# A mixture-of-experts layer on one core: rows kept in token order and fetched by a table, in place of rows scattered into expert order

## The chip, the core and the metric

The kernel runs on one core of a Trainium2 chip. The core has TensorE (PE in the profile; PEld is its weight load), VectorE (DVE), ScalarE (ACT), GpSimd (POOL) and SyncE (SP), each with its own instruction stream; they meet only at semaphores. 16 DMA engines serve all queues. The metric is the device time of one execution in microseconds; a kernel is compared by the median of its runs.

## What is computed

One layer: causal attention over a batch of 4 sequences of 1024 tokens and 256 channels, then a mixture of 8 experts. The part that matters here, with N = 4096 tokens:

```python
x = x + layernorm(attention(layernorm(x)))
xf = layernorm(x).reshape(-1, 256)
w, idx = top_k(xf @ Wg, 2);  w = softmax(w)              # two experts for each token
xhat = (xf - mean(xf)) * rsqrt(var(xf) + 1e-6)
h = relu((xhat * gamma[e] + beta[e]) @ W1[e] + b1[e])    # for each expert e
out[e] = h @ W2[e] + b2[e] + xf
y = sum over the token's two experts of w * out[e]
x = x + layernorm(y)
```

## The kernel before

The program is a row of stages, `project`, `attend`, `route` and `experts`, each a block at whose end all engines wait for one another. Everything that the change touches is in `route` and `experts`.

`route` works through the 4 sequences, called batches b, each of 8 tiles of 128 tokens (t). DVE takes the moments of the attention's output (L1034, L1038), POOL turns them into a reciprocal root and a shift with a power (`roots`, L997 to L1003), ACT applies these (`norm_y`, L1187), DVE adds the residual (L1044) and takes moments again, normalises into `xb` (`normalise`, L1053) and takes moments a third time. PE turns each tile (L1227), ACT copies it out of PSUM (`xfT`, L1195), PE multiplies it with the gate's weights (L1232). `pick_experts` on DVE (L1074 to L1098) finds each token's two experts, PE counts with triangular matmuls how many earlier tokens chose the same expert (`ps_r`, L1237 to L1242), and DVE gets each row's slot in the DRAM buffer `xs`. There each expert has a region of N + 256 rows. POOL then scatters the normalised rows `xh` into these slots: `scatter`, L1011, one indirect DMA of 128 rows for each tile and choice, 64 in all, cut in threes between the roots. Each row carries two more words: its token and the second expert. SP at last writes rows of zeros behind each expert's last row (L981), when the counts are known. DVE meanwhile works out how many tiles of 256 rows each expert has and where each begins in `xs` (L1148 to L1176: `base`, `tile_row`).

`experts` runs over the tiles i of 256 rows, expert after expert, 36 in this run. Tile i: SP has fetched its rows with one plain DMA (L1342) two tiles ahead, PE turns them (`turn`, L1464), ACT and DVE split them in two parts, PE does the first layer (L1477, 48 matmuls), turns the rows of the next tile, and does the second layer (L1488, 48 matmuls). DVE adds the bias into `o` (L1560), POOL reads the two extra words (L1407), works out each row's place in `ys` (L1416 to L1423), scatters `o` with two indirect DMAs (L1430) and waits for them to land. When an expert is done, SP refills the weights that it had used with the next but one expert's: `fill`, L1360, four DMAs of 1 MB. Every engine that loops reads nine loop bounds from `base` first (`firsts`, L1322). A last part reads `ys` back in token order and mixes.

The order is written by hand. POOL's queue in the routing holds roots and scatters in turn; SP's queue in `experts` holds the fetches and the refills.

## Time and profile before

| | us |
|---|---|
| median of 3 runs | 1285.25 (1284.64 to 1285.45) |
| the profiled execution's own time | 1283.42 |
| its span | 1281.8 |
| attention ends, routing begins | at 633.5 |
| experts' block begins | at 782.7 |
| first matmul of an expert | at 792.0 |
| last matmul of an expert | at 1215.6 |
| a tile of 256 rows | 11.72 |

In the rows, a line of the timeline is: start in us from the span's start, duration, engine, line of the kernel, operation, written tile <- read tiles, shapes, count, and in brackets the time for which the engine was idle before it and what ended that. An engine called SPq or POOLq is the queue's own record. A line of the groups has the busy time and the mean duration in ns of one. The granted clock of TensorE is 1.00 at 2.4 GHz and 0.50 at 1.2 GHz.

### The profile page before, as it was taken

The page shows a single profiled execution, that of the slowest core. Times are in us where ns is not written, and L with a number is a line of the kernel's source. Part 1 is how long each engine was busy: PE and PEld are TensorE (multiplying, and loading weights), DVE is VectorE, ACT ScalarE, POOL GpSimd, SP SyncE. Part 2 cuts the span into 40 slices and gives each one's busy share as a digit, 9 for nine tenths or more (in the row PEclk, how much of TensorE's full clock was granted, in tenths as well). Part 3 has the DMA queues.
Part 4 walks back from the last instruction along what each step waited for, and adds up shares of the span by engine and source line. Part 5 has one row for each costly group of instructions (what it writes and reads, how often), then busy time and mean ns, then how long its engine had stood idle before and what let it go on. Part 6 is the DMA issues. An engine that isn't in the chain of part 4 may idle for free. (4 is left out here: it accounts for less than half of the span.)

```text
span 1281.8 us, 24447 instructions
## 1 busy us (share of the span) xinstructions
PE 1054.5 (82%) x7329; PEld 806.4 (63%) x7329; DVE 824.1 (64%) x2492; ACT 640.9 (50%) x1111; POOL 588.2 (46%) x675
## 2 busy tenths in 40 slices
PE   5979999999999999998533513999999999999900
PEld 2545555555555555554233513999999999999900
DVE  6739877777777777772188521556655655565577
ACT  2640666666666666666444422444444544454533
POOL 4214555555555555556747771223222222232237
PEclk9985999999999999999855555999999999999955
DMA  4994344545444444432261235142541414421173
GB/s 147 372 359 131 107 167 167 167 167 167 165 165 160 159 160 160 169 113 108 96 236 66 83 128 196 59 162 63 183 178 48 177 49 177 146 79 50 41 270 131
DMA packets 93849, 190.03 MB, mean 148 GB/s; under 512 B 27480, under 2 KB 58600, under 8 KB 85512
## 3 DMA queue, kind: packets, MB, share of 16 engines
q1 hardware_dynamic: 84508, 165.14, 37.0%
q0 software_dynamic: 7680, 22.09, 5.0%
q10 hardware_dynamic: 1588, 1.92, 0.5%
q8 instruction: 34, 0.56, 0.2%
q14 instruction: 39, 0.32, 0.1%
HBM read 109.54 MB, written 79.05 MB: 147 GB/s over the span
## 5 line engine op out<-in xcount | busy, mean ns | idle before, releaser
L778 ACT ACTIVATE att_pt<-att_ps_s 128x1024 f32<-128x1024 f32 (+3 forms) x384 | 297.9, 814 | 180.5 <-PE att_ps_s L693 176.8
L805 DVE CUSTOM_DVE_ANT_0 att_ps_m<-att_ps_m,keep_future 128x384 f32<-128x384 f32 (+2 forms) x384 | 204.3, 586 | 77.9 <-PE att_ps_m L656 77.9
L1521 ACT ACTIVATE moe_hf<-moe_ps_h,moe_b 128x256 f32<-128x256 f32 x288 | 134.4, 474 | 224.7 <-PE moe_ps_h L1477 215.3
L656 PE MATMUL att_ps_m<-att_k,att_q 128*128 128x512 f32 (+3 forms) x576 | 181.1, 389 | 5.1 <-DVE att_pm L805 3.9
L814 DVE TENSOR_REDUCE att_pm<-att_ps_m 128x1 f32<-128x512 f32 x256 | 161.4, 685 | 21.8 <-PE att_ps_m L656 21.7
L601 POOL TENSOR_SCALAR_AFFINE_SELECT att_pt<-att_pt 128x512 f32<-128x512 f32 x128 | 81.3, 636 | 186.8 <-ACT att_pt L778 186.8
L693 PE MATMUL att_ps_s<-att_q,att_k 128*128 128x512 f32 (+3 forms) x576 | 156.0, 360 | 6.3 <-ACT att_pt L778 5.2
L1430 POOL DMA_INDIRECT ys<-moe_o,moe_home x72 | 74.1, 1029 | 183.3 <-DVE moe_o L1560 170.4
L693 PEld LDWEIGHTS att_ps_s<-att_q,att_k 128*128 128x128 f32 x576 | 95.2, 188 | 56.5 <-issue 28.9
L1554 DVE TENSOR_TENSOR moe_hTl<-moe_hf,moe_hTh 128x256 fp32r<-128x256 f32 x288 | 124.1, 431 | 10.0 <-DVE moe_hTh L1552 0.2
L656 PEld LDWEIGHTS att_ps_m<-att_k,att_q 128*128 128x128 f32 x576 | 99.7, 195 | 47.9 <-DVE att_pm L805 15.1
L591 POOL TENSOR_TENSOR att_rec<-att_sums,att_minus 128x16 f32<-128x16 f32 x33 | 95.9, 2905 | 31.8 <-ACT att_sums L764 31.8
L710 PE MATMUL att_ps_o<-att_pt,att_v 128*17 128x512 f32 (+3 forms) x1152 | 107.1, 488 | 3.7 <-ACTq L746 3.1
L1552 DVE CAST moe_hTh<-moe_hf 128x256 fp32r<-128x256 f32 x288 | 84.3, 293 | 33.1 <-ACT moe_hf L1521 29.5
L1560 DVE TENSOR_TENSOR moe_o<-moe_ps_o,moe_b 128x256 f32<-128x256 f32 x72 | 27.2, 419 | 110.0 <-PE moe_ps_o L1488 110.0
L1477 PE MATMUL moe_ps_h<-moe_xTh,weights_w_0h 128*128 128x256 f32 x288 | 81.7, 284 | 5.4 <-issue 5.4
L1488 PE MATMUL moe_ps_o<-moe_w2h,moe_hTh 128*128 128x256 f32 x288 | 82.0, 285 | 0.0
L1488 PE MATMUL moe_ps_o<-weights_w_0h,moe_hTh 128*128 128x256 f32 x288 | 82.0, 285 | 0.0
L1477 PE MATMUL moe_ps_h<-moe_xTh,weights_w_0l 128*128 128x256 f32 x288 | 81.5, 283 | 0.0
L1477 PE MATMUL moe_ps_h<-moe_xTl,weights_w_0h 128*128 128x256 f32 x288 | 81.5, 283 | 0.0
L1477 PE MATMUL moe_ps_h<-moe_xTh,moe_w1l 128*128 128x256 f32 x288 | 80.9, 281 | 0.0
L1477 PE MATMUL moe_ps_h<-moe_xTl,moe_w1h 128*128 128x256 f32 x288 | 80.9, 281 | 0.0
(197 smaller groups left out, 2503.8 us busy)
## 6 DMA issues: line engine op xcount, KB each, us to landing
att_raw<-in_w SPq DMA_DIRECT2D x16, 1024.0 KB, 5.3
ws<-att_raw_hi SPq DMA_DIRECT2D x16, 1024.0 KB, 3.9
ws<-att_raw SPq DMA_DIRECT2D x16, 1024.0 KB, 5.8
moe_rows<-xs SPq DMA_DIRECT2D x38, 258.0 KB
att_q<-qs SPq DMA_DIRECT2D x33, 256.0 KB
att_k<-ks SPq DMA_DIRECT2D x66, 128.0 KB
weights_w_0h<-ws SPq DMA_DIRECT2D x8, 1024.0 KB
weights_w_0l<-ws SPq DMA_DIRECT2D x8, 1024.0 KB
```

Of the source, the lines that this page charges most:

```text
L591: pool.tensor_tensor(rec[:, c], got[:, :, :, HS], minus[:], ALU.pow).then_inc(rec_done, 1)
L656: ins = pe.matmul(out[:, end - keys:end], qg[slot][:, h // 2, i * P:(i + 1) * P], kg[slot][:, h, k0:k0 + keys], start=not whole, stop=not ...
L693: ins = pe.matmul(out[:, e, off:CH], kg[slot][:, 2 * p + e, j * P:(j + 1) * P], qg[slot][:, p, c * CH + off:(c + 1) * CH], start=True, sto ...
L710: ins = pe.matmul(ps_o[32 * h:32 * h + VW, off:CH], vg[slot][:, j, h * VW:(h + 1) * VW], pt[:, blk % NPT, h, off:CH], start=(j == 0), stop ...
L778: act.activation(pt[:, blk % NPT, 2 * p:2 * p + 2, off:CH], ps_s[k % 2][:, :, off:CH], ACT.Exp, scale=HS ** -0.5).then_inc(ex_done, 1)
L805: ins = dve.tensor_tensor_reduce(part, part, future[:, CH - keys:CH], 1.0, LOWEST, ALU.add, ALU.max, pm[:, g % 2, 0, head, place:place + 1])
L814: return dve.tensor_reduce(pm[:, g % 2, 0, h, place:place + 1], src, AX.X, ALU.max)
L1477: ins = pe.matmul(ps_h[f % NHB][:], w1[r][a][:, k, f * P:(f + 1) * P], xT[m][:, k], start=(n == 0), stop=(n == 3 * CT - 1))
L1488: ins = pe.matmul(ps_o[t][:], hT[a][:, f, t * P:(t + 1) * P], w2[r][m][:, f], start=(f == 0 and (a, m) == pieces[0]), stop=(f == FT - 1 an ...
L1521: act.activation(hf[:, f % NHB], ps_h[f % NHB][:], ACT.Relu, bias=b1[r][:, f:f + 1]).then_inc(hf_done, 1)
L1552: dve.tensor_copy(hT[0][:, f], hf[:, f % NHB]).then_inc(hh_done, 1)
L1554: dve.tensor_tensor(hT[1][:, f], hf[:, f % NHB], hT[0][:, f], ALU.subtract).then_inc(hl_done, 1)
```

## The change

Rows are kept in token order. ACT writes `xh` as before, but SP stores it with one plain DMA for each batch in `xs`, now N + 128 rows of 256 words (the last 128 are zeros). No row is scattered in the routing and no region is padded.

In place of that, a table tells for each slot of each expert which row belongs there. Each expert has 34 columns of 128 slots (`TABLE`), 272 in all. A row's rank among its expert's rows is split on DVE into `low` (the last seven bits, the partition) and `high` (the column). For each tile and choice, `make_low` compares the numbers 0 to 127 with `low` (a one-hot row of 128 for each token), and `make_block` compares 0 to 271 with `cell`, the column. Both are done by POOL, 16 + 16 instructions for each batch; of the last batch DVE does the 16 of `make_low` and 8 of the 16 of `make_block`. ACT multiplies the first by the row's number in two parts (`rows_of`: 2 activations of 1024 columns and 8 of 256 for each batch), and PE adds up 32 matmuls of 272 columns for each batch in one PSUM bank (`table`). At the end DVE turns the sum into `home` (where the result goes) and `token` (which row to fetch), in 6 instructions.

In `experts`, POOL fetches the rows: it loads the tile's column number into a register, copies two columns of `token`, and gathers with two indirect DMAs (`gather`). It does so for tile i + 2 ahead of the scatter of tile i. SP no longer fetches, and its refills follow each other in its queue.

The routing is also rearranged: the second normalisation's moments are derived from the first (DVE's `normalise` and its third `moments` are gone; ACT does both normalisations in `norm_x`, straight from the head tiles), the copy L1204 is gone, moments are taken two batches ahead, and the loops over batches are written out.

POOL's queue in the routing. Before, around the last batches' roots:

```order
L1003 TENSOR_TENSOR route_shift<-route_nmean,route_rstd 128x8
L1011 DMA xs<-route_xh,route_slot 34816x258 x11
L997 TENSOR_SCALAR route_veps<-route_mv 128x8
L999 TENSOR_SCALAR route_nmean<-route_mv 128x8
L1001 TENSOR_TENSOR route_rstd<-route_veps,route_mhalf 128x8
L1003 TENSOR_TENSOR route_shift<-route_nmean,route_rstd 128x8
L1011 DMA xs<-route_xh,route_slot 34816x258 x27
```

After, from the roots of batch 2's `norm_y` to those of batch 3's:

```order
L1024 TENSOR_TENSOR route_shift<-route_nmean,route_rstd 128x8
L963 TENSOR_SCALAR route_at_low<-route_cols,route_low 128x128 x16
L969 TENSOR_SCALAR route_at_block<-route_cols,route_cell 128x272 x16
L1031 TENSOR_SCALAR route_veps<-route_mv 128x8
L1032 TENSOR_SCALAR route_veps<-route_mv 128x8
L1034 TENSOR_SCALAR route_nmean<-route_mv 128x8
L1036 TENSOR_TENSOR route_rstd<-route_veps,route_mhalf 128x16
L1038 TENSOR_TENSOR route_shift<-route_nmean,route_rstd 128x16
L1019 TENSOR_SCALAR route_veps<-route_mv 128x8
L1020 TENSOR_SCALAR route_nmean<-route_mv 128x8
L1022 TENSOR_TENSOR route_rstd<-route_veps,route_mhalf 128x8
```

The scatters behind a batch's roots have become comparisons, 16 and 16, and the roots of the next two normalisations stand behind them. On ACT `rows_of` of batch b stands behind `norm_y` of batch b + 3 and ahead of `norm_x` of batch b + 2.

SP's queue at the start of `experts`. Before:

```order
L1342 DMA moe_rows<-xs 128x2x258
L1338 TENSOR_LOAD keep_tile_row
L1338 ISA x2
L1342 ISA
L1342 DMA moe_rows<-xs 128x2x258
L1351 DMA moe_b<-in_b 128x8
L1353 DMA moe_b<-in_b 128x256
L1360 DMA moe_w1h<-ws 128x2048
```

After:

```order
L1410 DMA moe_b<-in_b 128x8
L1412 DMA moe_b<-in_b 128x256
L1419 DMA moe_w1h<-ws 128x2048
L1419 DMA moe_w1l<-ws 128x2048
L1419 DMA moe_w2h<-ws 128x2048
```

The two fetches that stood ahead of the second expert's weights on SP are now gathers on POOL; nothing stands ahead of the weights but the biases.

POOL's queue in one tile of the experts' loop, from the wait for the turned rows on. Before:

```order
L1416 TENSOR_SCALAR moe_chosen<-moe_tag,keep_ei 128x2
L1418 ISA
L1420 TENSOR_TENSOR moe_place<-moe_chosen,moe_tag 128x2
L1421 REGISTER_ALU
L1423 CAST moe_home<-moe_place 128x2
L1424 REGISTER_ALU
L1405 ISA
L1407 COPY moe_tag<-moe_rows 128x4
L1427 ISA
L1430 DMA ys<-moe_o,moe_home 8704x256 x2
L1432 ISA
```

After (the copy of `home`, with a register load of its own, stands ahead of these):

```order
L1480 REGISTER_ALU
L1482 ISA
L1456 ISA
L1456 TENSOR_LOAD keep_tile_row
L1456 ISA x2
L1462 ISA
L1462 COPY moe_source<-keep_token 128x2
L1463 REGISTER_ALU
L1466 DMA moe_rows<-xs,moe_source 128x256 x2
L1485 ISA
L1488 DMA ys<-moe_o,moe_home 8704x256 x2
L1490 REGISTER_ALU
```

The gather now stands ahead of the tile's scatter, and behind the wait for the scatter of the tile before, which closes the loop's body.

The diff, cut to its core:

```diff
+        def make_low(eng, b):
+
+            if b > 0:
+
+                eng.wait_ge(rows_done, b * LOW_ROWS)
+            for k in range(K):
+                for t in range(TB):
+                    ins = eng.tensor_scalar(at_low[:, k, t], cols[:, 0:P], low[:, k, t:t + 1], None, ALU.is_equal)
+            ins.then_inc(low_done, 1)
+
+        def make_block(eng, k):
+
+            for t in range(TB):
+                ins = eng.tensor_scalar(at_block[:, k, t], cols[:], cell[:, k, t:t + 1], None, ALU.is_equal)
+            ins.then_inc(block_done, 1)
...
-                sp.wait_ge(homes, 2)
-                sp.wait_ge(pad_known, 1)
-                settle(sp, keep["passed"])
-                for e in range(E):
-                    row = sp.value_load(pad[0:1, e:e + 1], min_val=e * CAP, max_val=e * CAP + N)
-                    sp.dma_start(d["xs"][bass.ds(row, XT), :].rearrange("(k p) c -> p k c", p=P),
-                                 zeros[:]).then_inc(padded, 16)
-                sp.wait_ge(padded, 16 * E)
+                sp.dma_start(d["xs"][N:N + P, :], zeros[:]).then_inc(kept, 16)
+                for b in range(B):
+                    sp.wait_ge(xh_done, b + 1)
+                    sp.dma_start(d["xs"][b * T:(b + 1) * T, :].rearrange("(k p) c -> p k c", p=P),
+                                 xh[:, b * TB:(b + 1) * TB]).then_inc(kept, 16)
+                sp.wait_ge(kept, 16 * (B + 1))
...
-                roots(0, 0)
-                roots(1, 1)
-
-                cuts = (0, 5, 10, K * TB)
-                for b in range(-1, B - 1):
-                    for n, (norm, ahead) in enumerate(((0, 2), (2, 1), (1, 2))):
-                        if b + ahead < B:
-                            roots(norm, 3 * (b + 1) + 2 + n if b + 2 < B else 3 * B - 1)
-                        if b >= 0:
-                            scatter(b, cuts[n], cuts[n + 1])
-                scatter(B - 1, 0, K * TB)
-                pool.wait_ge(scattered, 16 * K * TILES)
...
+                def table(b):
+
+                    pool.wait_ge(parted, b + 1)
+                    if b < B - 1:
+                        make_low(pool, b)
+                    if b > 0:
+
+                        pool.wait_ge(tabled, b)
+                    for k in range(K if b < B - 1 else K // 2):
+                        make_block(pool, k)
+
+                roots_y(0)
+                roots_y(1)
+                roots_x(0)
+                roots_x(1)
+                pool.wait_ge(c_in, 16 * 9)
+                for b in range(B):
+                    if b + 2 < B:
+                        roots_y(b + 2)
+                    table(b)
+                    if b + 2 < B:
+                        roots_x(b + 2)
...
-                        ins = dve.tensor_tensor(hit[:, k], pick[:, k], place[:], ALU.mult)
+                        ins = dve.tensor_tensor(hit[:, k], pick[:, k], ps_r[:], ALU.mult)
                     then(ins)
-                    then(dve.tensor_reduce(slot_f[:], hit[:], AX.X, ALU.add))
-                    dve.tensor_copy(slot[:, :, bass.ds(b * TB, TB)], slot_f[:]).then_inc(slots_in, 1)
+                    then(dve.tensor_reduce(rank[:], hit[:], AX.X, ALU.add))
+                    then(dve.tensor_copy(rank_i[:], rank[:]))
+                    then(dve.tensor_scalar(rank_i[:], rank_i[:], P.bit_length() - 1, None, ALU.logical_shift_right))
+                    then(dve.tensor_copy(high[:], rank_i[:]))
+                    if b > 0:
+
+                        dve.wait_ge(low_done, b)
+                        dve.wait_ge(block_done, b * K)
+                    dve.scalar_tensor_tensor(low[:], high[:], float(-P), rank[:], ALU.mult, ALU.add)
+                    then(dve.scalar_tensor_tensor(cell[:], which[:], float(TABLE), high[:], ALU.mult, ALU.add))
+                    dve.nop().then_inc(parted, 1)
                     then(dve.tensor_reduce(part[:], taken[:].rearrange("p t e -> p e t"), AX.X, ALU.add))
...
+                dve.wait_ge(tabled, B)
+                table = ps_tab[:, 0:E * TABLE]
+                then(dve.tensor_scalar(free[:], table, 0.0, None, ALU.is_equal))
+                then(dve.tensor_tensor(spare[:].rearrange("p (n k) -> p n k", k=2), free[:].rearrange("p (n k) -> p n k", k=2),
+                                       own_row[:, K:2 * K].unsqueeze(1).to_broadcast([P, E * TABLE // 2, 2]), ALU.mult))
+                then(dve.scalar_tensor_tensor(keep["home"][:], table, -1.0, spare[:], ALU.add, ALU.add))
+                then(dve.tensor_copy(token_i[:], keep["home"][:]))
+                then(dve.tensor_scalar(token_i[:], token_i[:], K.bit_length() - 1, None, ALU.logical_shift_right))
+                then(dve.tensor_copy(keep["token"][:], token_i[:]))
...
+                def norm_x(b):
+                    act.wait_ge(x_rs, b + 1)
                     settle(act, keep["passed"])
                     for t in range(TB):
-                        act.activation(by_group(yn, t), head_tile(b, t), ACT.Identity, scale=rstd[:, 0, t:t + 1],
-                                       bias=shift[:, 0, t:t + 1]).then_inc(yn_done, 1)
-
-                def keep_batch(b, call):
+                        act.activation(by_group(xf, b * TB + t), head_tile(b, t), ACT.Identity, scale=rstd[:, b, 1, t:t + 1],
+                                       bias=shift[:, b, 1, t:t + 1]).then_inc(xf_done, 1)
+                        if t > 0:
+                            keep_turned(b, t - 1)
+                    keep_turned(b, TB - 1)
                     for t in range(TB):
+                        ins = act.activation(by_group(xh, b * TB + t), head_tile(b, t), ACT.Identity,
+                                             scale=rstd[:, b, 2, t:t + 1], bias=shift[:, b, 2, t:t + 1])
+                    ins.then_inc(xh_done, 1)
...
+                def rows_of(b):
+
+                    act.wait_ge(low_done, b + 1)
+                    if b > 0:
+
+                        act.wait_ge(tabled, b)
+                    for k in range(K):
+                        act.activation(low_row[:, k], at_low[:, k], ACT.Copy, scale=own_row[:, k:k + 1]).then_inc(rows_done, 1)
                     for t in range(TB):
-                        ins = act.activation(tile(xh, b, t)[:, 0:C], xb[:, t], ACT.Identity, scale=rstd[:, 2, t:t + 1],
-                                             bias=shift[:, 2, t:t + 1])
-                    ins.then_inc(xh_done, 1)
-
-                    act.wait_ge(xh_done, b + 1)
-                    act.activation(xf[:, bass.ds(b * TB, TB), :], xb[:], ACT.Copy).then_inc(xf_kept, 1)
-
-                norm_y(0, 0)
-                with act.Fori(0, B - 1) as b:
-
-                    act.wait_ge(x1_done, b * TB + TB)
-                    norm_y(b + 1, b * 3 + 2)
-                    keep_batch(b, b * 3 + 3)
-                keep_batch(B - 1, 3 * B - 1)
+                        act.activation(low_tile[:, :, t], at_low[:, :, t], ACT.Copy, scale=float(K * P * (b * TB + t))
+                                       ).then_inc(rows_done, 1)
+
+                norm_y(0)
+                norm_y(1)
+                act.wait_ge(c_in, 16 * 9)
+                for b in range(B):
+                    norm_x(b)
+                    if b + 2 < B:
+                        norm_y(b + 2)
+                    if b > 0:
+                        rows_of(b - 1)
+                rows_of(B - 1)
...
+                def table(b):
+
+                    pe.wait_ge(block_done, (b + 1) * K)
+                    out = ps_tab[:, 0:E * TABLE]
+                    for k in range(K):
+                        pe.wait_ge(rows_done, b * LOW_ROWS + k + 1)
+                        for t in range(TB):
+                            pe.matmul(out, low_row[:, k, t], at_block[:, k, t], start=(b + k + t == 0), stop=False)
+                    for t in range(TB):
+                        pe.wait_ge(rows_done, b * LOW_ROWS + K + t + 1)
+                        for k in range(K):
+                            ins = pe.matmul(out, low_tile[:, k, t], at_block[:, k, t], start=False,
+                                            stop=(b == B - 1 and t == TB - 1 and k == K - 1))
+                    ins.then_inc(tabled, 1)
...
-                fetch(d["xs"][0:XT, :].rearrange("(k p) c -> p k c", p=P))
-                second = tile_slots(1)
-                sp.wait_ge(turned, 1)
-                sp.wait_ge(tagged, 1)
-                fetch(second)
...
-                def tile(q, r, i):
-                    ahead = tile_slots(i + 2)
-
-                    sp.wait_ge(turned, i + 2)
-                    sp.wait_ge(tagged, i + 2)
-                    fetch(ahead)
-
...
-                def read_tag(n):
-
-                    pool.wait_ge(rows_in, n * 16)
+                def columns(n):
+
+                    place = pool.value_load(keep["tile_row"][0:1, bass.ds(n, 1) if not isinstance(n, int) else slice(n, n + 1)],
+                                            min_val=0, max_val=E * TABLE // 2 - 1)
+                    return bass.ds(place * 2, 2)
+
+                def gather(n):
+
+                    pool.tensor_copy(source[:], keep["token"][:, columns(n)]).then_inc(sourced, 1)
+                    pool.wait_ge(sourced, n + 1)
                     settle(pool, keep["passed"])
-                    pool.tensor_copy(tag[:], rows[:, :, C:ROW]).then_inc(tagged, 1)
+                    for t in range(XT // P):
+                        pool.indirect_dma_start(rows[:, t], None, d["xs"],
+                                                bass.IndirectOffsetOnAxis(ap=source[:, t:t + 1], axis=0)).then_inc(rows_in, 16)
 
                 pool.memset(mhalf[:], -0.5).then_inc(consts, 1)
-                read_tag(1)
+                gather(0)
+                pool.wait_ge(turned, 1)
+                pool.wait_ge(rows_in, 32)
+                gather(1)
-                    pool.wait_ge(tagged, i + 1)
+                    pool.tensor_copy(home[:], keep["home"][:, columns(i)]).then_inc(homed, 1)
+                    pool.wait_ge(homed, i + 1)
                     settle(pool, keep["passed"])
...
```

## Rows read from the trace of the kernel before

**Rows 1.** Busy time by stretch: us; PE, PEld, DVE, ACT, POOL; granted clock.
```profile
633.50:782.70 149.20, 45.32 (x238) 41.47 (x238) 84.30 (x432) 51.29 (x101) 94.37 (x116) 0.50 0.36 128
...
792.30:794.70 2.40, 2.40 (x12) 2.40 (x12) 0.12 (x1) 0.47 (x1) 0.19 (x1) 0.50 0.93 382
...
792.00:1215.70 423.70, 423.60 (x3600) 423.39 (x3600) 246.87 (x683) 197.76 (x406) 114.25 (x212) 1.00 0.33 116
```

**Rows 2.** POOL's last scatter: start, us, instruction, idle before.
```profile
773.23 0.96 POOL L1011 DMA_INDIRECT xs<-route_xh,route_slot  x1 [0.30 <-issue]
```

**Rows 3.** POOL's group of the scatters.
```profile
L1011 POOL DMA_INDIRECT xs<-route_xh,route_slot x64 | 62.7, 980 | 23.1 <-issue 20.0 <-DVE route_slot L1096 3.1
```

**Rows 4.** SP's own queue: the padding, the first and the second refill.
```profile
748.79 31.56 SPq L981 DMA_DIRECT2D xs<-route_zeros  x8
...
788.19 0.43 SPq L1360 DMA_DIRECT2D moe_w1h<-ws  x1
...
853.10 0.35 SPq L1360 DMA_DIRECT2D weights_w_0h<-ws  x1
```

**Rows 5.** Chain that ended last: the first fetch and a later turn.
```profile
782.72 2.70 DMA moe_rows<-xs
...
869.61 0.44 PE moe_ps_x L1464 x4
```

**Rows 6.** DVE in time: moments of batch 0; its last row.
```profile
648.02 0.64 DVE L1038 BATCH_NORM_AGGREGATE route_mv<-route_stats 128x2 f32<-128x6 f32 x8
...
753.24 0.19 DVE L1176 CAST keep_tile_row<-route_ps_t 1x42 int32<-1x42 f32 x1
```

**Rows 7.** ACT and DVE in time: a normalisation, first turned tiles, their picking.
```profile
640.46 4.04 ACT L1187 ACTIVATE route_yn<-keep_y,route_shift,route_rstd 128x256 f32<-128x256 f32 x8 [10.86 <-POOL route_shift L1003]
...
659.10 0.63 ACT L1195 ACTIVATE route_xfT<-route_ps_x 128x256 f32<-128x256 f32 x2
668.58 0.69 DVE L1074 MAX8 route_best<-route_ps_g 128x8 f32<-128x8 f32 x8
...
673.59 0.17 DVE L1096 CAST route_slot<-route_slot_f 128x16 f32 x1
```

**Rows 8.** ACT's groups in the routing: busy us, mean ns, idle before.
```profile
L1195 ACT ACTIVATE route_xfT<-route_ps_x 128x256 f32<-128x256 f32 x32 | 11.8, 379 | 30.2 <-PE route_ps_x L1227 18.0 <-remote 6.8 <-PE route_ps_g L1232 4.0
...
L1204 ACT ACTIVATE keep_xf<-route_xb 128x2048 f32 x3 | 5.7, 1911 | 0.4
```

**Rows 9.** POOL's groups by shape over the whole program.
```profile
L591 POOL TENSOR_TENSOR att_rec<-att_sums,att_minus 128x16 f32<-128x16 f32 x33 | 95.9, 2905 | 31.8 <-ACT att_sums L764 31.8
...
L601 POOL TENSOR_SCALAR_AFFINE_SELECT att_pt<-att_pt 128x512 f32<-128x512 f32 x128 | 81.3, 636 | 186.8 <-ACT att_pt L778 186.8
...
L613 POOL TENSOR_TENSOR att_raw<-att_raw,att_raw_hi 128x1024 fp32r<-128x1024 f32 x32 | 75.6, 2385 | 0.0
```

**Rows 10.** One addition of DVE and the POOL instruction that started beside it.
```profile
658.16 2.74 DVE L1044 TENSOR_TENSOR keep_y<-keep_xf,route_yn 128x256 f32<-128x256 f32 x8
658.45 2.56 POOL L997 TENSOR_SCALAR route_veps<-route_mv 128x8 f32<-128x8 f32 x1 [3.52 <-DVE route_mv L1038]
```

**Rows 11.** First instruction of POOL and of PE in the experts' loop.
```profile
791.12 0.30 POOL L1416 TENSOR_SCALAR moe_chosen<-moe_tag,keep_ei 128x2 f32<-128x2 f32 x1 [5.35 <-issue]
792.00 0.57 PE L1477 MATMUL moe_ps_h<-moe_xTh,weights_w_0h 128*128 128x256 f32 x1 [5.43 <-issue]
```

**Rows 12.** POOL in an ordinary tile and in two with a refill.
```profile
846.51 0.69 POOL L1416 TENSOR_SCALAR moe_chosen<-moe_tag,keep_ei 128x2 f32<-128x2 f32 x1 [2.10 <-DMA ys<-moe_o,moe_home]
...
855.17 0.97 POOL L1430 DMA_INDIRECT ys<-moe_o,moe_home  x1 [0.30 <-issue]
...
863.68 0.29 POOL L1416 TENSOR_SCALAR moe_chosen<-moe_tag,keep_ei 128x2 f32<-128x2 f32 x1 [7.55 <-DMA ys<-moe_o,moe_home]
1073.42 0.28 POOL L1416 TENSOR_SCALAR moe_chosen<-moe_tag,keep_ei 128x2 f32<-128x2 f32 x1 [6.29 <-DMA ys<-moe_o,moe_home]
```

More of the change, by code:

```diff
@@ L1005, in scatter @@
-                def scatter(b, first, last):
-                    pool.wait_ge(slots_in, b + 1)
-                    pool.wait_ge(xh_done, b + 1)
-                    for n in range(first, last):
-                        t, k = b * TB + n // K, n % K
-                        pool.indirect_dma_start(d["xs"], bass.IndirectOffsetOnAxis(ap=slot[:, k, t:t + 1], axis=0),
-                                                xh[:, t, :], None).then_inc(scattered, 16)
-                roots(0, 0)
-                roots(1, 1)
@@ L1213, in _ @@
+                norm_y(0)
+                norm_y(1)
+                act.wait_ge(c_in, 16 * 9)
+                for b in range(B):
+                    norm_x(b)
+                    if b + 2 < B:
+                        norm_y(b + 2)
+                    if b > 0:
+                        rows_of(b - 1)
+                rows_of(B - 1)
                 act.wait_ge(weights_in, 1)
@@ L1384, in _ @@
                 first = firsts(sp)
-                each(sp, first, lambda q, r: None, tile, leave)
-                sp.wait_ge(rows_in, first[E] * 16 + 32)
-                settle(sp, keep["passed"])
+                for e in range(E):
+                    leave(e // 2, e % 2)
                 sp.wait_ge(o_free, first[E] + 1)
@@ L1434, in tile @@
                     pool.nop().then_inc(o_free, 1)
-                each(pool, firsts(pool), lambda q, r: None, tile)
+                first = firsts(pool)
+                each(pool, first, lambda q, r: None, tile)
+                pool.wait_ge(rows_in, first[E] * 32 + 64)
+                settle(pool, keep["passed"])
                 pool.wait_ge(consts, 1)
```

237 lines of the change are left out of this document (117 added, 120 removed).

## The prediction, made before the changed kernel ran

> **What bounds the kernel now.** I read the busy time by stretch first, to find which stages have an engine that is full [rows 1]. From 792.0 to 1215.7 PE is busy for 423.6 of 423.7 us: there only what makes PE wait can count, and a tile costs 11.72. In the routing, 633.5 to 782.7, nobody is full: POOL, the busiest, works 94.4 of 149.2 us, and PE runs at the lower clock (0.50). So the routing is a chain, and its end must be looked up. POOL issues its last scatter at 773.23 [rows 2] and the next block's first fetch starts at 782.72 [rows 5]; SP writes its padding from 748.79 for 31.56 us, so to 780.35 [rows 4]. The 64 scatters cost 62.7 us busy and 23.1 idle [rows 3]. DVE had its last result at 753.24 [rows 6]. The routing thus ends some 29 us after its arithmetic, for scatters and padding alone. Between 782.7 and the first matmul lie 9.3 us: the first fetch, 2.70 [rows 5], and on PE, behind the turn, 5.43 of reading loop bounds [rows 11], nine of them, so 0.6 each.
>
> **The routing after the change.** The scatters (62.7) and the padding go, and the stores in token order hide: SP is free and waits only for `xh`. What ends last has to be built up anew. I put the new steps on the old clock.
>
> *Batch 0.* DVE is done with moments at 648.7 [rows 6]. POOL's `roots_x` is three small steps of about 0.33, a power of 128x16, 2.9 [rows 9], and a shift: 4.2 with the waits, 652.8. ACT's `norm_x` alternates normalisations (4.04 for eight, 0.50 each [rows 7]) with the copies of turned tiles. Before, first copy to picking took 668.58 - 659.10 = 9.5 [rows 7]; with 1.3 ahead of the first copy the picking starts 10.8 after `roots_x`, at 663.6. ACT's last copy is 1.4 earlier, and eight rows of `xh`, 4.0, follow: 13.4 for one `norm_x`. In ACT's order, `norm_x` 0 (to 666.2), `norm_y` 2 (4.0), `norm_x` 1 (13.4), it is busy to about 683.7.
>
> *POOL's table.* The picking took 5.2 from its first step to the slots (668.58 to 673.59 + 0.17 [rows 7]); three steps more and one fewer make 5.5, so POOL may start at 669.1. The trace shows no comparison with a scalar from memory. Cheap end: one-input work of POOL without overhead; dear end: its two-input work. The affine select of 128x512 took 0.636 [rows 9], 1.07 ns an element above a fixed 0.09; the 128x2 operation with such a scalar took 0.30 [rows 11]. A comparison of 128 is then 0.40 with both and 0.26 without the scalar's overhead, one of 272 0.55 or 0.33 (bf16 output, taken at half). At the two-input slope, 2.385 for 1024 [rows 9], 2.3 ns an element, they would be 0.57 and 0.89. I take 0.40 and 0.55, since the select is a one-input operation with a comparison in it, like these. A batch costs POOL 16 x 0.40 + 16 x 0.55 = 15.2, and 2.8 more because DVE's additions lie beside it: an addition that took 2.74 for eight held a POOL step of some 0.24 for 2.56 [rows 10]. So 18.0, to 687.1.
>
> The Trainium skill says the same as that row: in "SBUF — State Buffer", section "Who interferes with whom", a DVE instruction with two SBUF inputs and a GpSimd instruction that reads SBUF exclude each other. But "GPSIMD Engine Reference", section "Performance pitfalls for Q7 kernels", gives a loop body that compares and then selects 2.03 cycles an element where it isn't unrolled and 1.03 where it is; by the first, at its 1.2 GHz, an estimate is 0.50 and 0.75, and the sum would be about 13 us worse. The select of 636 ns for 512 elements speaks for the second.
>
> *The rest of the chain.* Behind the table stand `roots_x` 2 and `roots_y` 3, 4.2 + 2.6, to 693.9: here ACT waits about 10 us for POOL, a new wait. Then ACT alone: `norm_y` 3 4.0 (698.0); `rows_of` 0, which is 2 activations of 1024 at 1.07 (half of the 1911 ns for 2048 [rows 8], with a little over) and 8 of 256 at 0.50, so 6.2 (704.2); `norm_x` 2 14.9, with 1.5 for PE's table matmuls, which may stand in front of its turns (719.1); `rows_of` 1 (725.2); `norm_x` 3 (740.1), whose picking is done at about 743; `rows_of` 2 (746.3), on which DVE's last `at_low` waits. DVE makes the last `at_low` (16 x 0.21, between the 0.17 of a step of 16 elements [rows 7] and the 0.34 of an addition of 256 [rows 10]) at 749.7. `at_block` waits for PE's table 2, to about 748.5; POOL 8 x 0.55 + 2.0 of the lock, 754.9. PE then needs 32 matmuls of 272 columns; 12 of 256 took 2.40 at clock 0.50 [rows 1], so 0.22 each, 7.0, 761.9; the loop's bounds (DVE's sums, PE's products in fp32) end about 764.8; six last steps of DVE 2.0, the block's end 1.0: **767.8**. Against 782.7 that is **-14.9**. DVE's two dropped passes and ACT's dropped copy (5.7 busy [rows 8]) are in this chain, not beside it. The ends: with the cheap comparisons POOL is never late and the block ends at 759, -23.7; with the dear ones at 792, +9.3. The gain is gone when a pair (one comparison of each kind) costs 1.1 instead of 0.95.
>
> **The experts' start.** SP's fetch becomes work of POOL: a register (0.6), a copy of two columns with its settling (about 1.0), two indirect DMAs at 0.96 + 0.30 (less the last's gap, 2.3) and a landing of 2.1 after the last issue [rows 12], 6.1 with the memset, where 2.7 stood. That is +3.4. But the DMAs of the second expert's weights, 4 MB, stood behind two fetches (first issue at 788.19 [rows 4]); now SP issues them about 1 us after the block begins, 1 us ahead of the gather. In the refilled tile the same happened to a scatter: refill issued at 853.10, scatter at 855.17 and before, landed 7.55 after its issue instead of 2.10 [rows 4, 12]. If the gather suffers so, +8.7. I take +7.0, nearer to the dear end since the order is the same. "DMA: Bandwidth & Descriptors" of the Trainium skill, section "Issuing engines are not separate DMA queues", holds that DMAs of all issuers run on the same 16 engines and interleave; rows 12 bear that out.
>
> **In the loop.** The gather of tile i + 2 takes POOL 2 registers, 2 copies and 2 indirect DMAs, 4.9, then 2.1 of landing: 7.0 after the wait for the tile before. In an ordinary tile that wait ends at 846.51 [rows 12], so the rows land at 853.5; PE turns them one tile (11.72) before 869.61 [rows 5], at 857.9. Hidden, with 4.4 to spare. What hides it is the wait for the stores being short. In a tile with a refill it ends at 863.68: landing 870.7, against the turn at 869.61, 1.1 late. There are six refills; their waits lie between 7.55 and 6.29 [rows 12], the lateness between 1.1 and nothing: **+3.2** in all (0 where PE's start is a little later in its tile; 8 if the refill slows the gather too). The tile's own length, PE's matmuls and the last part (1215.7 to the end) stay.
>
> **Sum.** -14.9 + 7.0 + 3.2 = -4.7. The profiled execution took 1283.42, so 1278.7; the median of the runs stands 1.8 above the profiled one: **1280.5**.
>
> **The rivals.**
> (1) POOL's comparisons are cheap. For it: the scalar's overhead may lie in the 128x2 operation itself. The routing ends at 759: -23.7 + 7.0 + 3.2 = -13.5, 1271.7; with an undisturbed first gather 1268. Chance 0.25.
> (2) Slower: POOL becomes what bounds the routing. Every batch's table stands in front of the roots that ACT needs (batches 2 and 3), so each us more in a table moves `norm_y` 3 and all behind it. For it: two-input slope [rows 9] and the lock [rows 10], which I counted at 2.8 a batch and may be more. It decides from a pair of 1.1 on; at 0.57 + 0.89 it is 9.3 + 7.0 + 3.2 = +19.5, 1304.8. Chance 0.27, most of it below 1298.
> (3) The forecast's prices, with the start and loop costs anywhere between their ends (3.4 to 8.7, and 0 to 8): 1274 to 1288. Chance 0.43.
> (4) The change doesn't bring what it removes, for another reason: before ACT's copies of turned tiles 6.8 us of idle are put down to "remote" [rows 8], which is no wait of the program; with the loops written out it may come at more places. At 9 us more, 1289.5. Chance 0.05.
>
> **Chances.** A measurement of this kernel can tell about 0.2%, 2.6 us. Below 1282.7 lie rival 1 (0.25) and most of the forecast's case (0.29): faster 0.54. Within 1282.7 to 1287.8: 0.12 of the forecast's case, 0.05 of rival 2: 0.17. Above: 0.29. The range leaves 0.1 at either side: from 1266 (cheap comparisons, first gather undisturbed, nothing lost in the loop) to 1298 (pair of 1.3). The likeliest case's own range is 1274 to 1288.
>
> **What would show it.** In the changed kernel's profile: the experts' block begins at 767.8 (right), 759 or 792; POOL's groups of `at_low` and `at_block` have means of 400 and 550 ns, or 260 and 330, or more; ACT is idle before `norm_y` of batch 3 for about 10 us, ended by POOL; the 32 matmuls of a table take about 7; the first gather lands 7.0 to 11.4 after the block begins and the first matmul comes 16 after it; PE waits in the loop at the turns of six tiles for some 0.5 each and nowhere else; a tile stays 11.72. The forecast is wrong if the comparisons' price is outside 0.85 to 1.1 for a pair, if a wait that I haven't named holds ACT or DVE in the routing, or if PE waits for rows in ordinary tiles.

## The result

The changed kernel takes 1309.8 us (median of 4 runs, 1308.5 to 1311.7) against 1285.3: slower, ratio 1.0191, 95% interval 1.0178 to 1.0203. The forecast was 1280.5 with a range from 1266 to 1298. The profiled execution's own time is 1309.55, its span 1307.8; before it was 1283.42 and 1281.8.

| stretch of the profiled execution | before | forecast | changed kernel |
|---|---|---|---|
| routing begins (DVE's first moments) to experts' block | 148.7 | 133.8 | 154.3 |
| block's begin to the first matmul | 9.3 | 16.3 | 17.4 |
| first to last matmul of the experts | 423.6 | 426.8 | 435.5 |
| the rest | 66.1 | 66.1 | 66.1 |

The first three rows make +5.6, +8.1 and +11.9, the routing itself begins 0.5 later: 26.1, where the spans differ by 26.0. Every stretch that the change touches became longer; none gave back what the other took.

Busy time by stretch in the changed kernel, in the columns of [rows 1]:

```profile
633.50:788.70 155.20, 59.75 (x366) 49.78 (x366) 77.69 (x369) 76.55 (x169) 108.08 (x145) 0.59 0.25 84
806.10:1241.70 435.60, 430.28 (x3600) 428.84 (x3600) 248.44 (x683) 195.40 (x406) 161.24 (x214) 0.99 0.29 102
```

POOL lost its 62.7 us of scatters and is busier than before, 108.1 us instead of 94.4. In the experts' loop PE, which had been idle for 0.1 us, is idle for 5.3, and its same 3600 matmuls fill 430.3 us instead of 423.6. POOL's two new groups in the routing (count, busy us, mean ns, idle before):

```profile
L969 POOL TENSOR_SCALAR route_at_block<-route_cols,route_cell 128x272 bf16<-128x272 f32 x56 | 53.0, 982 | 5.5 <-PE route_ps_tab L1288 5.5
L963 POOL TENSOR_SCALAR route_at_low<-route_cols,route_low 128x128 bf16<-128x128 f32 x48 | 29.3, 636 | 16.5 <-ACT route_low_tile L1256 8.9 <-DVEq L1135 7.7
```

POOL in time, and who waits for it (start, us, instruction, idle before):

```profile
712.43 9.33 POOL L963 TENSOR_SCALAR route_at_low<-route_cols,route_low 128x128 bf16<-128x128 f32 x16 [8.87 <-ACT route_low_tile L1256]
721.72 15.08 POOL L969 TENSOR_SCALAR route_at_block<-route_cols,route_cell 128x272 bf16<-128x272 f32 x16
...
703.68 4.04 ACT L1224 ACTIVATE route_yn<-keep_y,route_shift,route_rstd 128x256 f32<-128x256 f32 x8 [18.21 <-POOL route_shift L1024]
741.15 1.09 ACT L1231 ACTIVATE keep_xf<-keep_y,route_shift,route_rstd 128x256 f32<-128x256 f32 x2 [11.76 <-POOL route_shift L1038]
770.83 2.19 ACT L1254 ACTIVATE route_low_row<-route_at_low,route_own_row 128x1024 bf16<-128x1024 bf16 x2 [13.59 <-PE route_ps_tab L1288]
```

Sixteen `at_low` take 9.33 us, 0.583 each; sixteen `at_block` 15.08, 0.942 each (from start to start; the means of the groups count overlaps twice). A pair costs 1.53 us, a batch 24.4. ACT waits 18.2 us for POOL's roots ahead of `norm_y` 3, 11.8 ahead of `norm_x` 3, and 13.6 for PE's table, which itself waits for `at_block`. The start of the experts, from the chain that ended last:

```profile
792.30 7.22 DMA moe_rows<-xs,moe_source
799.57 1.13 PE moe_ps_x L1525 x4
```

The first gather lands 7.22 us after its last issue, where the plain fetch took 2.70 [rows 5]. An ordinary tile in that chain, and a tile after a refill:

```profile
849.11 0.44 PE moe_ps_x L1525 x4
849.54 5.70 PE moe_ps_o L1549 x48
855.24 5.70 PE moe_ps_h L1538 x48
860.94 0.44 PE moe_ps_x L1525 x4
...
917.55 7.22 DMA ys<-moe_o,moe_home
...
929.66 2.66 DMA moe_rows<-xs,moe_source
...
932.58 0.66 PE moe_ps_x L1525 x4
```

From turn to turn an ordinary tile takes 11.83 us; before it was 11.72:

```profile
857.88 0.44 PE moe_ps_x L1464 x4
858.32 5.61 PE moe_ps_o L1488 x48
863.93 5.68 PE moe_ps_h L1477 x48
```

After the refill the chain leaves PE: the scatter lands 7.22 us after its last issue, and the gather's landing ends PE's wait. The first layers of the six tiles concerned are longer than the others by 0.2, 0.6, 0.7, 1.2, 0.6 and 3.0 us, 6.2 in all. In the longest, POOL pauses for 2.01 us between the two DMAs of the gather, where it is 0.30 in the other tiles. The trace puts the pause down to nothing in particular, and e1_low_dve, e2_roots_between, e3_fill_late and e12_same_places have it (2.0 to 2.2) at the same refill:

```profile
1145.11 1.19 POOL L1466 DMA_INDIRECT moe_rows<-xs,moe_source  x1 [0.82 <-POOL moe_source L1462]
1148.31 1.04 POOL L1466 DMA_INDIRECT moe_rows<-xs,moe_source  x1 [2.01 <-issue]
```

Behind this stall the granted clock is lower for a while, and the second layer takes 6.50 instead of 5.70:

```profile
1139.90:1147.60 7.70, 7.70 (x67) 7.70 (x66) 4.23 (x13) 2.85 (x6) 1.61 (x3) 1.00 0.69 273
1151.20:1158.80 7.60, 7.59 (x54) 7.60 (x55) 0.69 (x1) 1.65 (x3) 2.61 (x5) 0.82 0.10 35
```

The loop's 11.9 us are thus some 7.5 of stalls with what hangs on them, 36 times 0.11 (3.9) of slower matmuls, and 0.5 at the start and end.

### The profile page after: what moved, and what is told of

It is laid out like the page before. It is cut to its first block and busy times, and to the rows that moved or that the text cites. A ratio compares the mean times of both kernels' runs of the same rounds, so it can differ in the third digit from the quotient of the medians.

```text
span 1307.8 us, 24358 instructions
## 1 busy us (share of the span) xinstructions
PE 1075.7 (82%) x7457; PEld 820.2 (63%) x7457; DVE 819.1 (63%) x2429; ACT 663.9 (51%) x1179; POOL 652.7 (50%) x709
## 5 line engine op out<-in xcount | busy, mean ns | idle before, releaser
L1466 POOL DMA_INDIRECT moe_rows<-xs,moe_source x76 | 76.0, 1001 | 44.5 <-POOL moe_source L1462 31.2
L1549 PE MATMUL moe_ps_o<-weights_w_0l,moe_hTh 128*128 128x256 f32 x288 | 81.5, 283 | 0.0
```

The source lines that it names most:

```text
L1549: ins = pe.matmul(ps_o[t][:], hT[a][:, f, t * P:(t + 1) * P], w2[r][m][:, f], start=(f == 0 and (a, m) == pieces[0]), stop=(f == FT - 1 an ...
```

## The experiments

Four questions were open: is it POOL's comparisons that lengthen the routing (and not the new hand-overs); what delays the first gather; what makes the stalls in the loop; and why PE's own matmuls come slower.

### The routing: POOL's work or its place

```diff
-                    if b < B - 1:
-                        make_low(pool, b)
...
                     if b + 2 < B:
                         residual(b + 2)
-
-                make_low(dve, B - 1)
+                    make_low(dve, b)
```

> The changed kernel with make_low of every batch on DVE (behind the batch's residual) in place of POOL; make_block stays. Theory POOL's comparisons are too dear (0.583 + 0.942 a pair) and its queue holds back ACT: POOL loses 3 x 9.3 us, ACT's waits of 18.2 and 11.8 us for POOL's roots shrink to under 9 and 3, and the experts' block begins at about 765.5 instead of 788.7; total about 1309.8 - 23 = 1287. Rival, the new hand-overs (table on PE, rows_of on ACT, single buffers) set the pace and not POOL's work: the block begins after 780, total above 1301. Start of the experts (17.5 us) and their loop (435.5) unchanged in both.

Measured: 1287.7 us, 1.0022 of the kernel before (1.0012 to 1.0032). The routing takes 130.8 us instead of 154.3, 23.5 less, where 23.2 were expected; start (17.3) and loop (435.5) stayed. ACT's waits for POOL fell from 18.2 and 11.8 to 8.8 and 5.4 (under 9 and 3 were expected):

```profile
696.77 4.04 ACT L1222 ACTIVATE route_yn<-keep_y,route_shift,route_rstd 128x256 f32<-128x256 f32 x8 [8.82 <-POOL route_shift L1024]
727.77 1.09 ACT L1229 ACTIVATE keep_xf<-keep_y,route_shift,route_rstd 128x256 f32<-128x256 f32 x2 [5.44 <-POOL route_shift L1038]
```

So 28 us of comparisons taken from POOL are worth 23.5: its load was what the routing waited for. The other edit keeps the load and moves only the roots:

```diff
                     if b < B - 1:
                         make_low(pool, b)
+                    if b + 2 < B:
+                        roots_x(b + 2)
+                    if b == 0:
+                        roots_y(3)
                     if b > 0:
...
-                for b in range(B):
-                    if b + 2 < B:
-                        roots_y(b + 2)
-                    table(b)
-                    if b + 2 < B:
-                        roots_x(b + 2)
+                roots_y(2)
+                for b in range(B):
+                    table(b)
```

> The changed kernel with only POOL's order altered: roots_x of batches 2 and 3 and roots_y of batch 3 stand between a table's at_low and at_block comparisons, not behind both. POOL's work is the same. Theory POOL's load: ACT's wait for norm_y of batch 3 is 15 us shorter, but tables and turned tiles still queue behind POOL's comparisons, so the block begins at about 780 (9 us earlier), total 1301. Rival, the place of the roots alone is what costs: begins below 772, total below 1293. Rival, the place is nothing: 787 to 789.

Measured: 1306.4, the routing takes 149.9, 4.4 less: about half of the 9 expected, and between that and the rival by which the place is nothing. What POOL waited for between its first comparison and its last wait for PE:

```profile
POOL route_at_low L963 <- DVEq L1136: 8.8, 3, 7.7
```

Of these 8.8 us 7.7 lie ahead of the first comparison. From 672.8 to 760.5 POOL then has nothing but 1.1 us of waits: with the roots out of the way the comparisons stand end to end, and moving the roots can't hide them. Two of the three groups of sixteen `at_low` took over 10.5 here beside DVE's additions, as in [rows 10], where one did in the changed kernel. That is 1.2 of the 4.6 us that are missing; the rest stays open.

### What the comparison costs

The kernel with 80 more operations on POOL behind its last comparison, eight of each kind, each kind behind the one before:

```diff
+                for n, price in enumerate((
+                        lambda t: pool.tensor_scalar(out_b[:, t], cols[:], cell[:, 0, t:t + 1], None, ALU.is_equal),
+                        lambda t: pool.tensor_scalar(out_b[:, t], cols[:], five, None, ALU.is_equal),
...
+                        lambda t: pool.tensor_copy(out_f[:, t], cols[:]),
+                        lambda t: pool.tensor_scalar(out_b[:, t], in_b[:], cell[:, 0, t:t + 1], None, ALU.is_equal),
+                        lambda t: pool.tensor_tensor(out_f[:, t], cols[:], cols[:], ALU.add),
```

> The changed kernel with 80 more operations on POOL behind its last comparison, eight of each kind on 128x272: comparison with a scalar from memory or an immediate, bf16 or fp32 out, product, copy, bf16 in, and an addition of two tiles. Theory the comparison's price of 0.94 us is that of every tensor_scalar of POOL, some 2.5 ns an element whatever the scalar: all six such groups at 0.85 to 0.95, the copies at 0.3 to 0.4, the addition at about 0.7. Rival, the scalar from memory costs: immediates at 0.6 or less. Rival, the bf16 output costs: fp32 outputs at 0.6 or less. Rival, the comparison: products at 0.6 or less. It prolongs the kernel by its own 60 us.

Measured in one execution, in time (the duration is that of all eight):

```profile
788.11 7.69 POOL L1073 TENSOR_SCALAR route_out_b<-route_cols,route_cell 128x272 bf16<-128x272 f32 x8
795.88 7.54 POOL L1074 TENSOR_SCALAR route_out_b<-route_cols 128x272 bf16<-128x272 f32 x8
803.52 7.55 POOL L1075 TENSOR_SCALAR route_out_f<-route_cols,route_cell 128x272 f32<-128x272 f32 x8
...
818.80 7.58 POOL L1077 TENSOR_SCALAR route_out_f<-route_cols,route_cell 128x272 f32<-128x272 f32 x8
826.47 7.56 POOL L1078 TENSOR_SCALAR route_out_f<-route_cols 128x272 f32<-128x272 f32 x8
...
837.09 2.92 POOL L1080 COPY route_out_f<-route_cols 128x272 f32<-128x272 f32 x8
840.11 7.55 POOL L1081 TENSOR_SCALAR route_out_b<-route_in_b,route_cell 128x272 bf16<-128x272 bf16 x8
847.74 4.82 POOL L1082 TENSOR_TENSOR route_out_f<-route_cols 128x272 f32<-128x272 f32 x8
```

There are seven kinds of `tensor_scalar`; all but the first (7.69) cost the same to 0.04 us in eight, 0.94 us each: comparison or product (L1077, L1078), scalar from memory or an immediate, bf16 or fp32 on either side. A copy costs 0.37 and an addition with two inputs (`cols` twice) 0.60. All three rivals (scalar, type, comparison) fall. It is the instruction: on POOL a `tensor_scalar` of 272 elements is here dearer by half than an addition with two inputs. With the 0.583 of the 128 elements it comes to 2.5 ns an element above 0.26. The affine select of [rows 9], 636 ns for 512 elements, so at most 1.24 ns an element, is another instruction, and says nothing of it.

### The first gather

```diff
                 biases(0, 0)
+                sp.wait_ge(rows_in, 32)
                 fill(0, 1)
```

> The changed kernel in which SP waits for the first gather's landing before it issues the second expert's weights (4 MB). Theory the weights' packets stand in front of the gather's: it lands about 2.1 to 2.7 us after its last issue instead of 7.2, and the first matmul comes 12.5 to 13 us after the block's begin instead of 17.5; total about 1305. The second gather takes the delay instead, about 5 us, hidden behind the first tile. Rival, an indirect gather from DRAM is slow by itself: landing stays near 7, total 1310.

Measured: 1307.1, and the first matmul comes 13.0 us after the block's begin instead of 17.4. From its chain:

```profile
794.39 2.79 DMA moe_rows<-xs,moe_source
```

The landing went from 7.22 to 2.79 with nothing changed but 4 MB of weights issued behind it. A gather isn't slow by itself. The routing of this run began 1.9 us later than in the changed kernel's profile, so that its span shows only half of the gain of 4.4; the loop is unchanged (435.5).

### The stalls in the loop

```diff
-                    pool.tensor_copy(home[:], keep["home"][:, columns(i)]).then_inc(homed, 1)
-                    pool.wait_ge(homed, i + 1)
-                    settle(pool, keep["passed"])
                     pool.wait_ge(turned, i + 2)
...
                     gather(i + 2)
+                    pool.wait_ge(stored, i * 32 + 32)
+                    settle(pool, keep["passed"])
+                    pool.tensor_copy(home[:], keep["home"][:, columns(i)]).then_inc(homed, 1)
+                    pool.nop().then_inc(o_free, 1)
...
-                    pool.wait_ge(stored, i * 32 + 32)
-                    settle(pool, keep["passed"])
-                    pool.nop().then_inc(o_free, 1)
```

> The changed kernel in whose loop POOL gathers tile i + 2 ahead of the wait for the scatter of tile i - 1, not behind it (two small loads at the start give the semaphore its first count). Theory the stalls at the turns of refilled tiles come from the scatter's slow landing (7.2 to 7.8 us) standing in front of the gather: the stalls of 0.2, 0.6, 0.7, 1.2, 0.6 and 3.0 us in PE's first layers and the 1.3 us of a lower clock behind the last vanish, the loop is about 7.5 us shorter (428 instead of 435.5), total about 1302. Rival, the gather itself is slowed by the refill: PE waits for rows in the same six tiles by 1 us or more, total above 1307. A tile's other matmuls keep 11.84 us in both.

Measured: 1293.5, twice the expected gain. All six stalls are gone, though the tiles are shorter, and PE waits for rows at no turn but the first: the wait for the scatter in front of the gather was their cause. But the loop went from 435.5 to 418.2, 17.3 less, of which the stalls are 7.5. The rest is in the tiles, which the expectation had held at 11.84:

```profile
851.33 0.44 PE moe_ps_x L1531 x4
851.77 5.66 PE moe_ps_o L1555 x48
857.42 5.46 PE moe_ps_h L1544 x48
862.88 0.44 PE moe_ps_x L1531 x4
```

11.55 us, and PE's instructions are the same. What else had changed was the place of its operands: the two loads that give the semaphore its first count need 64 bytes a partition, allocated ahead of `xg`, so `xT`, `hT` and the buffers about them lie 64 bytes further on.

### The pace of PE's matmuls

The changed kernel with that space alone, and no other edit:

```diff
+        s.sb("space", [P, 16])
         xg = s.sb("xg", [P, CT, XT])
```

> The changed kernel with 64 unused bytes a partition allocated ahead of xg, so that xTh, xTl, hTh and hTl start at a multiple of 128 bytes instead of 64 behind one; no instruction differs. Theory the pace of the experts' matmuls hangs on where their operands lie in SBUF: a matmul of the first layer comes every 113 ns instead of 119, one of the second every 118 instead of 119, a tile takes 11.55 us instead of 11.84, total about 1309.8 - 10 = 1300; the stalls in tiles with a refill stay. Rival, the pace in e4_gather_first came from POOL's other order: tile 11.84 and 1309.8 here.

Measured: 1306.5. The tiles are at 11.55 us (layers of 5.46 and 5.66), as in e4_gather_first, so the place did it. The total is 3.3 us better and not 10: faster tiles leave POOL less time, and the stalls behind refills grew, so that the loop is 429.9. The reverse, on the kernel before: its `xT` and `hT` moved by 32 bytes, and all operands at multiples of 512.

> The kernel before with 32 unused bytes a partition ahead of xg, so that its xT and hT lie as in the changed kernel (64 bytes behind a multiple of 128, where they lay 32). Theory placement: a tile takes 11.84 us instead of 11.72, a matmul comes every 118.8 ns, total about 4 us longer than before (1289). Rival, the gathers (their DMAs into rows or their instructions) slow PE: no difference here, 1285.

> The kernel before with 320 unused bytes ahead of the first weights and 288 ahead of xg, so that weights, xT and hT all start at multiples of 512 bytes. Theory placement, both operands count: each layer at 113 ns a matmul or below, tile 11.1 to 11.3 us, total 1265 to 1272. Rival, only the alignment of xT and hT counts: first layer 113, second 118, tile 11.55, total about 1279. Rival, no effect of placement: 1285.

Measured: 1293.6 and 1293.7, both 0.6% slower than before (intervals 1.0044 to 1.0078 and 1.0042 to 1.0076). A tile takes 11.93 and 11.95. In e7_before_space32:

```profile
848.09 0.44 PE moe_ps_x L1465 x4
848.52 5.75 PE moe_ps_o L1489 x48
854.27 5.76 PE moe_ps_h L1478 x48
860.02 0.44 PE moe_ps_x L1465 x4
```

So 32 unused bytes cost the kernel before 8 us. But the place of `xT` and `hT` that I expected to give the changed kernel's pace gave a slower one (the weights had stayed where they were), and full alignment, expected to be the best, is the slowest: alignment isn't what counts. The last test of the cause gives the changed kernel the places of before, weights and operands exactly 4096 bytes further on:

> The changed kernel with 1920 unused bytes ahead of the first weights and 96 ahead of xg, so that all weights, xT and hT lie exactly 4096 bytes behind their places in the kernel before. Theory placement is the whole of the 0.12 us that a tile is longer: tile 11.72 again, with the same spacing of matmuls as before (117.3 and 117.0 ns), total about 4 us less, 1305.5; the stalls in tiles with a refill stay. Rival, the gathers or the changed code add it: 11.84 and 1309.8, or another value.

Measured: 1307.3, with a loop of 430.9 instead of 435.5. The tile is that of the kernel before, to within 0.01 us, in its total and in both layers:

```profile
849.99 0.44 PE moe_ps_x L1526 x4
850.42 5.61 PE moe_ps_o L1550 x48
856.03 5.68 PE moe_ps_h L1539 x48
861.71 0.44 PE moe_ps_x L1526 x4
```

The gathers and the new code thus don't slow PE in an ordinary tile. `home` and `token` in `keep`, and the fewer and smaller buffers ahead of `xg`, had moved its operands, and that is the 0.11 us a tile.

### A version that beats both, and a rule that fell

The three mends together (`make_low` and half of `make_block` of every batch on DVE, SP's weights behind the first gather, the gather ahead of the wait):

> The changed kernel with three causes mended at once: make_low and the second half of make_block of every batch on DVE; SP's first weights behind the first gather's landing; the loop's gather ahead of the wait for the scatter (this brings its 64 bytes of placement too, as in e4_gather_first). Theory the three are separate places of one chain and add up: routing shorter by 28 us (from the same arithmetic that gave 23 for make_low alone, now with 8 of 16 at_block too), start by 4.3, loop by 17.5, so 1309.8 - 50 = 1260 (1257 to 1265). Rival, DVE becomes what bounds the routing: its additions and comparisons in one queue keep the block's begin behind 770 (on a clock in which the routing starts at 634.5), total above 1269.

Measured: **1257.9 us**, 0.9775 of the kernel before (0.9762 to 0.9788). Routing 122.8, start 12.8, loop 418.9; the three add up as expected. POOL is no longer asked for more than it can give, and the version is 2.2% faster than the kernel before. Not all of that is due to the change: e9_three has the places of e5_space64, and its tile of 11.55 us is worth about 36 x 0.17 = 6 us against the 11.72 of before. The kernel before at that same pace is e11_before_placed below; against it the gain is 24.5 us, 1.9%.

```profile
633.50:758.70 125.20, 61.97 (x366) 50.69 (x366) 87.88 (x441) 76.41 (x169) 64.61 (x74) 0.60 0.31 104
771.50:1191.00 419.50, 418.91 (x3600) 418.71 (x3600) 244.54 (x684) 194.77 (x408) 173.20 (x215) 0.99 0.31 113
```

POOL's busy time in the routing is 64.6 us instead of 108.1, DVE's 87.9 instead of 77.7. Then a rule for the places was tried, the distance of the two operands:

> e9_three with 128 unused bytes ahead of hf, which moves only hT. So far the pace went with the distance of the moving from the stationary operand modulo 256 bytes: 192 gave 113.7 ns a matmul, 32 117.0, 64 118, 128 118.8, 224 117.3, 0 120. Theory that distance decides: the second layer (now at 192 like the first) goes from 118 to 113.7 ns, a tile from 11.55 to 11.34 us, total 8 to 10 us under e9_three. Rival, another property of the places: second layer between 116 and 120, total within 4 us of e9_three.

> The kernel before with 224 unused bytes ahead of xg and 128 ahead of hf, so that both layers have the distance 192 modulo 256 between their operands. Theory the distance decides: both layers at 113.7 ns, tile 11.34 instead of 11.72 us, total about 1285.3 - 14 = 1271. Rival, it doesn't: 1280 to 1294, as the other two placements of before gave 1293.6 and 1293.7.

Measured: 1258.1, no better than e9_three, and 1282.3, 0.9963 of before (0.9949 to 0.9977). In e11_before_placed a tile takes 11.56 us and not 11.34: the first layer 5.46, the second 5.66, with the same distance in both. In e10_three_placed the second layer did become 5.46 us, but the first went from 5.46 to 5.66, though only `hf`, `hT` and what lies behind them had moved, none of which PE reads there:

```profile
849.46 0.44 PE moe_ps_x L1531 x4
849.90 5.46 PE moe_ps_o L1555 x48
855.36 5.66 PE moe_ps_h L1544 x48
861.02 0.44 PE moe_ps_x L1531 x4
```

The rule has fallen with that. What in the places sets the pace stays open; other engines write `hf` and `hT` while the first layer runs, so it may lie with them, but that wasn't tried.

## Why the prediction was wrong

*Where the time is bound.* Right: routing a chain, experts bound by PE, tail unchanged (66.1 and 66.1).

*The routing, -14.9 forecast, +5.6 measured: 20.5 of the 30.7 us by which the spans miss.* The step that failed is the price of a comparison. I had two ends, 0.26 + 0.33 and 0.57 + 0.89, and took 0.40 + 0.55, "since the select is a one-input operation with a comparison in it, like these". It was 0.58 + 0.94, just above the dear end (e6_prices). The likeness was one of arithmetic, and the price belongs to the instruction. Nearest in kind was the 128x2 operation of [rows 11], a `tensor_scalar` itself, but with two elements it shows no slope; no row showed one. That POOL's load stands in the path is shown by e1_low_dve: 28 us less of it made the routing 23.5 shorter, where 23.2 were expected from the measured price. "The gain is gone when a pair costs 1.1 instead of 0.95" is a slip for the routing. With 48 pairs in the path its 14.9 us are gone at 1.26; what is gone by 1.1 (at 1.05) is the 4.7 of the whole sum. The forecast's own dear end gave 792 against 788.7: `rows_of` took 4.6 us and not 6.2 (its eight copies of 256 took 2.54 and not 4.0), and PE's mean clock in the routing was 0.59 instead of 0.50. The wait that I named, ACT ahead of `norm_y` 3, came at 18.2 instead of 10; the same cause made two more, ahead of `norm_x` 3 and of the last `rows_of`. The forecast had followed POOL through its first table only. At its own prices the second ends at 704.2 + 18.0 = 722.2 and the roots behind it at 726.4, already 1.2 later than ACT wants them, so it had no slack left for a dearer comparison.

*The rule that was weighed against it.* I had set a pair of 1.25 aside by the select's row; it was nearer to the measured 1.53 than what I took. It was an estimate by the 2.03 cycles an element that "GPSIMD Engine Reference" of the Trainium skill, section "Performance pitfalls for Q7 kernels", states for a loop that compares and selects. The measured slope of 2.5 ns is 3 cycles at the 1.2 GHz of that estimate, dearer than either of the two figures that the Trainium skill has there (e6_prices).

*The experts' start, +7.0 forecast, +8.1 measured.* Right in mechanism and nearly in size: landing 7.22, and 2.79 with the weights behind it (e3_fill_late).

*The loop, +3.2 forecast, +11.9 measured.* The mechanism, a gather behind the scatter's wait in refilled tiles, is shown by e4_gather_first, and ordinary tiles hid it as said. Two terms were mis-sized or missing. The stalls, counted as 3.2, were 6.2 and 1.3 more behind them: gather landings took 2.6 to 2.9 and not 2.1, and from the scatter's landing to the gather's it took 7.55 us (924.77 to 932.32), not 7.0; the last refill, at 3.0, stood out, 1.7 of it by the pause between POOL's two DMAs. And that "the tile's own length, PE's matmuls and the last part" stay was false for the first two: 3.9 us came from buffers that moved (e12_same_places). That no edit touches an instruction doesn't mean that nothing touches its time.

*The rivals.* Rival 2 was the one that came, in its mechanism, from the point named and nearly at its time (1304.8 with the pair at 1.46; without the moved buffers the changed kernel took 1307.3). The time is in part luck: its routing was 3.7 us too long, its loop 8.7 too short. I gave it 0.27 and then cut its range at 1298, "most of it below 1298", though its own worked-out end lay above. With an unknown price between two rows, the chance was spread over the cheap half on the strength of one likeness.

## What to carry to other kernels

Before work is moved to POOL, price the very instruction there, with its slope: a `tensor_scalar` isn't an addition, a copy or a select. Where an engine's queue holds both a long batch of work and the small steps that another engine waits for, its load goes straight on to the path as soon as the work doesn't fit between two of these steps. A prefetch belongs ahead of every wait for a store in its queue, and ahead of bulk loads on any queue. And when buffers are added or change size, compare the pace of an unchanged inner loop before and after, since the difference may be theirs.

## What the runs showed of the hardware that was not expected

- On POOL `tensor_scalar` of 128x272 takes 0.94 us for comparison and product alike, bf16 or fp32, scalar from memory or immediate; `tensor_tensor` 0.60, a copy 0.37.
- The same 96 matmuls and the turns of a tile took 11.56 to 11.95 us in the kernel before, and 11.55 to 11.83 in the changed one, with nothing changed but the SBUF addresses of the loop's buffers (e5_space64, e7_before_space32, e8_before_aligned, e11_before_placed, e12_same_places). 32 bytes were worth 8 us to the kernel before.
- A gather of 256 rows whose first DMA is issued 1.2 us behind the first of four 1 MB loads of weights (790.86 and 789.66) lands 7.2 us after its last issue; with the weights held back, 2.8 (e3_fill_late).
